# Interleaving the mask and score matmuls of two 64-column halves in a chunked attention kernel

## The chip, the cores and the metric

The kernel runs on one core of a Trainium2 chip. The metric is the device time of one execution in microseconds.

## The reference

Two layers, on x and ctx of shape 32 x 128 x 1024 (batch, channels, places). The first is attention within chunks of 64 places, 8 heads of 16 channels, then a projection, a residual and a normalisation over the places. The second finds for each place its 30 nearest places by the first channels of ctx, makes weights from their relative positions with a small network whose batch norms span everything, and adds the weighted neighbours' rows. Cut to what the change touches:

```python
qh, kh, vh = proj(q, Wq, bq), proj(k, Wk, bk), proj(v, Wv, bv)        # N, nc, 64, H, Dh
scores = jnp.einsum('bnqhd,bnkhd->bnhqk', qh, kh) * scale
km = masks[:, 0, :].reshape(N, nc, CHUNK)
scores = scores + jnp.where(km[:, :, None, None, :] > 0, 0.0, NEG)
attn = jax.nn.softmax(scores, axis=-1)
out = jnp.einsum('bnhqk,bnkhd->bnqhd', attn, vh)
...
pd = 2.0 * jnp.einsum('bdn,bdm->bnm', p, p) - xx[:, :, None] - xx[:, None, :]
idx = jax.lax.top_k(pd, k)[1]
```

## The kernel before

Three stages follow one another. Stage a (to about 4030 us of the span) loops over the 32 batches, and in a batch over 8 tiles t of 128 places (two chunks of 64 each). It computes the attention and the neighbour search together, by orders written out by hand for each engine, with semaphores between them. Stages b and e, the network and the weighted sum, do not touch the code of the change.

In stage a, VectorE (DVE) searches. For a pair of tiles it takes four rounds of 8 maxima over 1024 distances (MAX8 L866, FIND_INDEX8 L871, MATCH_REPLACE8 L873). In between it does, for the attention, the negated maximum of the scores (`largest`, L896), the reciprocal of the softmax sums (`inverse`, L900), and once in a half batch the digits of the indices (`digits`, L827 to L835). The distances stand in `pd_sb`, a ring of four tiles, which ScalarE (ACT) fills from PSUM in two halves a tile (L588).

TensorE (PE) walks per tile t through: the distances of tile t + 2, first half; second half; `scores` of tile t + 1; the transpose of tile t - 1's probabilities (L453); its values (L463); and on some tiles the output rows (L568), the value projection (L425), the query and key projection (L416) and the squares. Between these stand units of a neighbour gather for the batch before (L482, L503). So the distances of tile 7 come behind the scores of tile 5, those of tile 5 behind the scores of tile 3, and those of tile 3 behind the scores of tile 1. ACT walks through the same order, with the exponents (L754) between the two halves of the distances.

`scores(b, par, t)` waits for `exp_ready` (ACT has read the scores of the tile before, since `s_ps` is one bank) and for `kz_ready` (GpSimd, POOL, has spread the keys over the heads, L1115). It then makes four matmuls into `s_ps`, two for each half e of its 128 output partitions: a mask matmul of 32 rows x 64 columns in bf16 (L440), which starts the sum, and a score matmul of 128 rows x 64 columns in fp32 (L444), which adds to it. The last one raises `s_ready`, for which DVE's `largest` and POOL's key spreading two tiles on wait. The two halves use the same 32 or 128 rows, and different columns, of the array. An fp32 matmul stands in the trace as two records.

POOL spreads the keys of tile t + 1, multiplies the probabilities of tile t - 1 by the reciprocals (L1091), and does its share of the gather (L958 to L965) and of the spherical coordinates. At t = 3, from the third batch on, come 16 steps `sph_signs` (L987 to L1003) ahead of the spreading for tile 5.

Of the kernel before, what the change touches and what calls it, by code (L numbers as in the profile page):

```python
# [25 lines left out]
HEADS, CHUNK = 8, 64  # L26
# [7 lines left out]
QT = TILES // QUADS  # L34
# [111 lines left out]
def stage_a(nc, x, ctx, mask, w_in, b_in, w_out, b_out, consts, y_dram, cst, con, planes, idx_all, stats_all):  # L146
    OHR = 3
    XR = 97
    with ExitStack() as st:
        def sb(name, shape, dt=F32):  # L150
            return st.enter_context(nc.sbuf_tensor(name, shape, dt))
# [40 lines left out]
        qs = sb("qs", [P, HALF])  # L192
        kt = sb("kt", [P, HALF])
        kz = sb("kz", [P, 2, 2, HEADS, CHUNK])
# [11 lines left out]
        s_ps = st.enter_context(nc.psum_tensor("s_ps", [P, HEADS, CHUNK], F32))  # L206
# [154 lines left out]
        def _(pe):  # L361
            pe.wait_ge(w_in_landed, 96)
            for g in range(4):
                m = nc.tensor.transpose(mi_ps[0][:, g * C:(g + 1) * C], wnat[:, g, :], con["ident"])
# [64 lines left out]
            def scores(b, par, t):  # L429

                s = b * TILES + t

                if not (isinstance(s, int) and s == 0):
                    pe.wait_ge(exp_ready, s)
                pe.wait_ge(kz_ready, s + 1)
                if t == 0:
                    pe.wait_ge(minv_ready, b + 1)
                for e in range(2):
                    keys = minv[:, par, (2 * t + e) * CHUNK:(2 * t + e + 1) * CHUNK]
                    nc.tensor.matmul(s_ps[64 * e:64 * e + 64], negs[MASKS],  # L440
                                     keys.rearrange("p (o k) -> p o k", o=1).to_broadcast([32, HEADS, CHUNK]),
                                     start=True, stop=False)
                for e in range(2):
                    m = nc.tensor.matmul(s_ps[64 * e:64 * e + 64], qs[:, bass.ts(2 * (t % QT) + e, CHUNK)], kz[:, t % 2, e],  # L444
                                         start=False, stop=True)
                m.then_inc(s_ready, 1)

# [60 lines left out]
            def emit(b, j, par, first, last):  # L508
                misc = Misc(misc_base(b), first_bank(b, par))
                turned = None  # L510
                for t in range(TILES):
# [28 lines left out]
                    if quarter < QT - 1:  # L540
                        scores(b, par, t + 1)
                    elif ongoing:
                        scores(nb, npar, (t + 1) % TILES)
# [29 lines left out]
            for t in range(2):  # L573
                for h in range(2):
                    distances(0, 0, t, h)
            queries_keys(misc0, 0, 0)
            scores(0, 0, 0)
            batches(pe, emit)
            tail = Misc(TAIL, TAIL % 2)
# [1439 lines left out]
```

## Time and profile before

| what | value |
|---|---|
| median of 3 runs | 5792.33 us (5790.41 to 5798.28) |
| the profiled execution | 5790.41 us, span 5788.3 us |
| mean granted TensorE clock | 0.882 |
| busy share of the span | DVE 89%, PE 77%, ACT 70%, POOL 53%, PE weight loads 46% |

A PE at 77% is not 77% of its peak, since matmul ends are modelled and matmuls overlap. Busy shares are means over all three stages; what an edit costs is read from the waits in its own stage. L12 is line 12 of the kernel; PEld is TensorE's weight load.

### The profile page before, as it was taken

To read this page: it belongs to the slowest core of one execution; us is meant where nothing else is said; L and a number is where in the kernel's file an instruction comes from. 1 tells how busy PE (TensorE), PEld (TensorE's weight loads), DVE (VectorE), ACT (ScalarE), POOL (GpSimd) and SP (SyncE) were. 2 spreads that over 40 slices of the span, in tenths; PEclk is the share of its full clock that TensorE was granted. 3 is DMA by queue.
4 is the path that set the end of the run, shared out by engine and by line. 5 is a ranking of instruction groups with operands and counts; after the bars stand their busy time and mean duration, and the time that the engine had idled before them with its cause. 6 is when DMAs were issued, how large, how long until landed. Compare 5 with 4: busy or idle time off the path is not lost. (4 is left out here: it accounts for less than half of the span.)

```text
span 5788.3 us, 168890 instructions
## 1 busy us (share of the span) xinstructions
PE 4441.9 (77%) x62610; PEld 2689.3 (46%) x63182; DVE 5158.6 (89%) x7549; ACT 4026.4 (70%) x9505; POOL 3040.9 (53%) x3780
## 2 busy tenths in 40 slices
PE   6777777777777777777777777776395889899989
PEld 2444444444444444444444444443242666666666
DVE  7999999999989999998999998997398988888887
ACT  3777777777777777777777777776533766676666
POOL 3577777777777777777777777776400000000000
PEclk7988889888888898888888888897697999999999
DMA  0010000010000001000001000000000000000000
GB/s 29 16 31 16 16 17 17 17 31 16 17 16 17 17 17 31 16 17 16 17 17 31 17 16 17 16 16 12 1 0 8 25 30 27 30 26 30 27 30 26
DMA packets 135798, 114.60 MB, mean 20 GB/s; under 512 B 105344, under 2 KB 106112, under 8 KB 134784
## 3 DMA queue, kind: packets, MB, share of 16 engines
q1 hardware_dynamic: 134912, 102.73, 6.1%
q8 instruction: 563, 9.22, 0.7%
q14 instruction: 323, 2.65, 0.2%
HBM read 69.16 MB, written 33.55 MB: 18 GB/s over the span
## 5 line engine op out<-in xcount | busy, mean ns | idle before, releaser
L866 DVE MAX8 vals<-pd_sb 128x8 f32<-128x1024 f32 x1024 | 1199.8, 1210 | 270.2 <-ACT pd_sb L588 253.9
L588 ACT ACTIVATE ohT<-oh_ps 128x512 bf16<-128x512 f32 x1920 | 1152.2, 615 | 371.2 <-remote 209.7
L871 DVE FIND_INDEX8 idx<-vals,pd_sb 128x8 uint16<-128x1024 f32 x1024 | 1243.4, 1217 | 0.0
L503 PEld LDWEIGHTS g_ps<-tparts,ohT 128*128 128x128 bf16 x23040 | 871.6, 99 | 381.9 <-issue 152.4
L503 PE MATMUL g_ps<-tparts,ohT 128*128 128x24 bf16 x23040 | 883.4, 175 | 86.1 <-issue 46.9
L873 DVE MATCH_REPLACE8 pd_sb<-vals,pd_sb 128x1024 f32<-128x1024 f32 x768 | 927.4, 1207 | 0.0
L1955 PEld LDWEIGHTS e_a_ps<-planes,e_oh 120*128 120x128 bf16 x24576 | 687.2, 98 | 300.7 <-issue 219.8
L482 PE MATMUL oh_ps<-bitsT,code 128*128 128x512 bf16 x1348 | 584.2, 438 | 294.2 <-ACT bitsT L772 154.8
L1725 ACT COPY e_at<-e_a_ps 128x512 f32<-128x512 f32 x512 | 542.9, 1060 | 358.1 <-PE e_a_ps L1955 352.3
L1955 PE MATMUL e_a_ps<-planes,e_oh 120*128 120x32 bf16 x24576 | 702.4, 178 | 85.2 <-DVE e_oh L1883 46.9
L407 PE MATMUL pd_ps<-ctx_s 128*128 128x512 f32 x1024 | 656.1, 727 | 76.7 <-ACT pd_sb L588 74.8
L754 ACT ACTIVATE sS<-s_ps,mx 128x64 f32<-128x64 f32 x2048 | 609.0, 327 | 142.4 <-DVE mx L896 141.6
L1883 DVE TENSOR_TENSOR e_oh<-e_pairs,e_iotan 120x2048 bf16<-120x2048 bf16 x512 | 623.7, 1219 | 3.0 <-PE e_a_ps L1955 1.4
L482 PEld LDWEIGHTS oh_ps<-bitsT,code 128*128 128x128 bf16 x1920 | 193.7, 104 | 872.4 <-issue 396.9
L961 POOL TENSOR_TENSOR gsb<-gsb 128x240 f32<-128x240 f32 (+2 forms) x1152 | 543.4, 472 | 90.3
L1115 POOL TENSOR_TENSOR kz<-kt,cst 128x1024 f32<-128x1024 f32 x256 | 486.6, 1901 | 157.9 <-ACT kt L588 102.9
L1969 PE MATMUL e_o_ps<-e_at,e_xT 128*128 128x512 f32 x1024 | 568.3, 650 | 0.2 <-ACT e_at L1725 0.2
L1091 POOL TENSOR_TENSOR sS<-sS,rs 128x512 f32<-128x512 f32 x256 | 277.7, 1085 | 446.8 <-DVE rs L900 446.7
L440 PE MATMUL s_ps<-xp,negs 32*64 32x512 bf16 x512 | 115.1, 443 | 512.8 <-ACT sS L754 259.0
L588 ACT ACTIVATE pd_sb<-pd_ps,nxx 128x512 f32<-128x512 f32 x512 | 365.2, 713 | 198.5 <-PE pd_ps L409 198.3
L754 ACT ACTIVATION_READ_ACCUMULATOR sS<-s_ps,mx 128x1 f32 x2048 | 451.6, 221 | 0.0
L958 POOL TENSOR_TENSOR gsb<-gsb,hi1h 128x480 f32<-128x480 f32 x384 | 438.6, 1142 | 23.1 <-DVE hi1h L835 19.2
(241 smaller groups left out, 7381.1 us busy)
## 6 DMA issues: line engine op xcount, KB each, us to landing
ctx_s<-in_ctx SPq DMA_DIRECT2D x32, 512.0 KB, 4.3
maskb<-in_mask_Bx1x_ff SPq DMA_DIRECT2D x32, 512.0 KB, 6.4
x_s<-in_x SPq DMA_DIRECT2D x32, 512.0 KB, 5.7
y_spill<-y_s SPq DMA_DIRECT2D x32, 512.0 KB, 3.0
e_y<-y_spill SPq DMA_DIRECT2D x32, 512.0 KB, 4.1
out<-e_o SPq DMA_DIRECT2D x64, 256.0 KB, 2.2
table<-in_ctx SPq DMA_DIRECT2D x96, 4.0 KB, 5.8
pd_sb<-in_shape_constants SPq DMA_DIRECT2D x1, 1180.0 KB, 5.3
```

What stands on the lines that cost most here:

```text
L407: nc.tensor.matmul(pd_ps[:], ctx_s[:, par, bass.ts(t, P)], ctx_s[:, par, bass.ts(h, HALF)], start=True, stop=False)
L482: nc.tensor.matmul(oh_ps[k % 2][:], code[:, k % KT, :], bitsT[:, k // KT, :], start=True, stop=True).then_inc(oh_ready, 1)
L503: m = nc.tensor.matmul(found_ps[gi % 2][:, k % GK, t, :], ohT[:, k % OHR, bass.ts(t, P)], tparts[:, par, part, :], start=(part == 0), stop ...
L588: return nc.scalar.activation(dst, src, func, scale=scale, bias=bias)
L754: m = nc.scalar.activation(sS[:, t % 2, hd, :], s_ps[:, hd, :], ACT.Exp, bias=mx[:, t % 2, hd:hd + 1], accum_out=rs[:, t % 2, hd:hd + 1])
L866: nc.vector.max(vals[:, i, :], pd_sb[:, (t + i) % RING, :]).then_inc(topk_step, 1)
L871: found = nc.vector.max_index(idx16[:, par, t + i, 8 * r:8 * r + 8], vals[:, i, :], work)
L873: nc.vector.match_replace(work, vals[:, i, :], work, REMOVED).then_inc(topk_step, 1)
L961: steps(nc.gpsimd.tensor_tensor(sums[:, :, 0:width], sums[:, :, 0:width], sums[:, :, width:2 * width], ALU.add))
L1883: v.tensor_tensor(oh[pp, g % RING], low.to_broadcast([QCOLS, NB // 2, LO, 2]), row.to_broadcast([QCOLS, NB // 2, LO, 2]), ALU.is_equal).th ...
L1955: m = nc.tensor.matmul(a_ps[g % 2][:, i].rearrange("p t e -> p (t e)"), oh[pp, g % RING, i // 2, :, i % 2], spr[q][pp, part, :, (g * NB + ...
L1969: m = nc.tensor.matmul(o_ps[q][:], xT[:, par, e, :], at[:, q, e].rearrange("p t n -> p (t n)"), start=(e == 0), stop=(e == HI - 1))
```

## The change

Within `scores`, the four matmuls are issued in another order. Before: mask of half 0, mask of half 1, scores of half 0, scores of half 1. After: mask of half 0, scores of half 0, mask of half 1, scores of half 1. The operands, the waits and the semaphore on the last matmul stay.

```diff
                 for e in range(2):
+                    ch = 2 * (t % QT) + e
                     keys = minv[:, par, (2 * t + e) * CHUNK:(2 * t + e + 1) * CHUNK]
                     nc.tensor.matmul(s_ps[64 * e:64 * e + 64], negs[MASKS],
                                      keys.rearrange("p (o k) -> p o k", o=1).to_broadcast([32, HEADS, CHUNK]),
                                      start=True, stop=False)
-                for e in range(2):
-                    m = nc.tensor.matmul(s_ps[64 * e:64 * e + 64], qs[:, bass.ts(2 * (t % QT) + e, CHUNK)], kz[:, t % 2, e],
+                    m = nc.tensor.matmul(s_ps[64 * e:64 * e + 64], qs[:, bass.ts(ch, CHUNK)], kz[:, t % 2, e],
                                          start=False, stop=True)
                 m.then_inc(s_ready, 1)
```

## Rows read from the trace of the kernel before

**Rows 1.** The page: busy share of DVE in tenths, 40 slices of the span.
```profile
DVE  7999999999989999998999998997398988888887
```

**Rows 2.** Waits of DVE, 340 to 4030 us: total, times, longest.
```profile
DVE vals L866 <- ACT pd_sb L588: 226.6, 30, 8.4
```

**Rows 3.** Waits of PE in the same stretch, the two ahead of scores.
```profile
PE s_ps L440 <- POOL kz L1115: 248.1, 87, 5.4
PE s_ps L440 <- ACT sS L754: 217.7, 146, 3.6
```

**Rows 4.** Timeline of one call of scores (start, length): PE and PEld, 2000.3 to 2002.2.
```profile
2000.48 0.40 PE L440 MATMUL s_ps<-xp,negs 32*64 32x512 bf16 x2 [1.58 <-POOL kz L1115]
2000.81 0.20 PEld L444 LDWEIGHTS s_ps<-kz,qs 128*64 128x64 f32 x4 [0.23 <-issue]
2000.81 1.08 PE L444 MATMUL s_ps<-kz,qs 128*64 128x512 f32 x4
2001.82 0.10 PEld L482 LDWEIGHTS oh_ps<-bitsT,code 128*128 128x128 bf16 x1 [0.81 <-issue]
```

**Rows 5.** Timeline of one fp32 matmul of 128 x 128 x 512, PE.
```profile
2007.63 1.10 PE L407 MATMUL pd_ps<-ctx_s 128*128 128x512 f32 x2
```

**Rows 6.** Timeline, PE and PEld, elsewhere: shape kept, then shape changed.
```profile
2002.35 0.63 PE L453 MATMUL mi_ps<-cst,sS 128*128 128x128 f32 x4
2002.71 0.10 PEld L482 LDWEIGHTS oh_ps<-bitsT,code 128*128 128x128 bf16 x1
2002.82 0.38 PE L482 MATMUL oh_ps<-bitsT,code 128*128 128x512 bf16 x1
...
1973.74 1.35 PEld L425 LDWEIGHTS mi_ps<-wT,ctx_s 128*64 128x64 f32 x24 [0.76 <-issue]
```

**Rows 7.** Timeline of another call of scores (tile 6), PE and PEld.
```profile
1987.21 0.64 PE L440 MATMUL s_ps<-xp,negs 32*64 32x512 bf16 x2 [4.63 <-POOL kz L1115]
1989.68 0.10 PEld L482 LDWEIGHTS oh_ps<-bitsT,code 128*128 128x128 bf16 x1 [1.61 <-issue]
```

**Rows 8.** Timeline from the keys of tile 5 to DVE's wait, all engines.
```profile
1965.33 1.90 POOL L1115 TENSOR_TENSOR kz<-kt,cst 128x1024 f32<-128x1024 f32 x1 [0.25 <-POOL turn L1003]
1967.38 0.40 PE L440 MATMUL s_ps<-xp,negs 32*64 32x512 bf16 x2 [2.60 <-POOL kz L1115]
1969.58 0.60 ACT L588 ACTIVATE ohT<-oh_ps 128x512 bf16<-128x512 f32 x1 [2.79 <-remote]
1973.93 0.69 ACT L588 ACTIVATE y_s<-mi_ps,bias 128x512 f32<-128x512 f32 x1 [0.81 <-PE mi_ps L568]
1984.79 0.74 ACT L588 ACTIVATE pd_sb<-pd_ps,nxx 128x512 f32<-128x512 f32 x1
1985.67 1.23 DVE L866 MAX8 vals<-pd_sb 128x8 f32<-128x1024 f32 x1 [7.05 <-ACT pd_sb L588]
```

**Rows 9.** Stretch: busy PE, PEld, DVE, ACT, POOL, clock, DMA share, GB/s.
```profile
1968.80:1971.90 3.10, 2.77 (x47) 2.31 (x46) 3.10 (x5) 1.67 (x4) 2.68 (x6) 0.51 0.00 0
```

**Rows 10.** Timeline of the keys of tile 4, POOL.
```profile
1939.00 1.90 POOL L1115 TENSOR_TENSOR kz<-kt,cst 128x1024 f32<-128x1024 f32 x1 [2.47 <-ACT kt L588]
1942.31 1.04 POOL L1091 TENSOR_TENSOR sS<-sS,rs 128x512 f32<-128x512 f32 x1 [1.40 <-DVE rs L900]
1944.16 1.36 POOL L1125 CAST bitsb<-bits 128x896 bf16<-128x896 uint16 x1 [0.82 <-DVE bits L827]
```

**Rows 11.** Timeline: scores of tile 1, distances of tile 3, DVE's use of them.
```profile
1904.13 1.98 PE L444 MATMUL s_ps<-kz,qs 128*64 128x512 f32 x4
...
1918.56 0.74 ACT L588 ACTIVATE pd_sb<-pd_ps,nxx 128x512 f32<-128x512 f32 x1
...
1921.42 1.21 DVE L866 MAX8 vals<-pd_sb 128x8 f32<-128x1024 f32 x1
```

**Rows 12.** Timeline: DVE's maxima over the scores of tile 6.
```profile
1991.69 0.64 DVE L896 TENSOR_REDUCE mx<-s_ps 128x8 f32<-128x512 f32 x1
```

## The prediction

> **What bounds the kernel now.** I read the page first. Its slices of DVE [rows 1] show nine tenths or more in nearly every slice of stage a, so stage a is as long as DVE's work plus DVE's waits, and the change lies in stage a alone. The second view is the waits of DVE in stage a's steady part [rows 2]: one wait is left that matters, before the first maximum over a tile's distances, 226.6 us in 30 times, so 7.55 us each. Nothing on DVE waits for the scores themselves in this stretch. The third view, the timeline, says where in a batch the wait falls and what leads to it [rows 8]: it is the first use of tile 7's distances, and these come behind tile 5's scores on PE. The chain is: POOL ends its spherical steps, spreads the keys of tile 5 (start 1965.33, 1.90 us), PE starts the scores at 1967.38, ACT's next one-hot waits 2.79 us for PE, later its output rows wait 0.81 us for PE, and behind the value copies, one table load and eight exponents ACT ends the distances at 1985.53 (1984.79 + 0.74); DVE starts 0.14 us later. Each link waits for the one before, so a call of scores that takes longer here makes this wait longer by the same. It occurs once a batch, for the 30 batches in which POOL has the spherical steps (batches 2 to 31).
>
> The fourth view, the waits of PE [rows 3], says the opposite of the other calls. In 240 calls of this stretch PE stood waiting before the scores, 248.1 us for keys (87 times) and 217.7 us for ACT's exponents (146 times), both of which hang on DVE or POOL. There a longer call eats the slack of the next call's wait.
>
> **The change, part by part.** Nothing is added: four matmuls and the same weight loads stand in another order. What it can remove is overlap. Today's call [rows 4]: the two masks start together (one row, x2, 0.40 us long), the four score records begin 0.33 us later and are through 1.08 us after that, and the load that follows starts at 2001.82. So the call costs 2001.82 - 2000.48 = 1.34 us. The four score records are two fp32 matmuls of 64 columns; one of 128 columns takes 1.10 us alone [rows 5]. So the two halves run beside each other and one half alone would take as long as both.
>
> Do they still meet in the new order? Between the two score matmuls there now stands a mask matmul of another shape (32 rows, not 128). What the trace shows of a change of shape: where the shape stays, the next weights are loaded during the matmuls before (L482's load at 2002.71, while L453 runs, its own matmul at 2002.82, [rows 6]). Where it changes, they are not: L444's load starts 0.33 us after the masks' start and with its own matmul, after PEld had stood idle 0.23 us; L482's after the scores with 0.81 us idle [rows 4]; L425's (64 columns, after 128) with 0.76 us idle [rows 6]. All are put down to "issue", that is, to nothing that a semaphore shows. I read this as PE emptying itself before it changes shape. In the new order the shape changes after every matmul, so nothing overlaps: mask 0.33, scores 1.01, mask 0.33, scores 1.01, together 2.68 us. The cost of a call is +1.34 us at the full clock (2.4 GHz). The same call at the half clock (1.2 GHz) takes 1989.68 - 1987.21 = 2.47 us [rows 7], so there it costs up to +2.47 us.
>
> The Trainium skill says the same in "TensorEngine Tiling (Array Packing)", Key Properties: changing the tiling mode, not just the tile, drains TensorE. By that rule the halves cannot meet and each call costs its own length again. The trace agrees, by the idle weight loads above.
>
> *On the path.* The 30 calls for tile 5: 30 x 1.34 = 40.2 us, if PE is at the full clock; 30 x 2.47 = 74.1 us at the half clock. In the batch shown the clock was 0.51 from 1968.8 to 1971.9 [rows 9], just behind the call. I take 40.2: if the slow stretch lies where it lay, the added work fills a part of it and pushes the same amount of other PE work to where the clock is full, so the end of the chain moves by the full-clock price.
>
> *Two places with little slack.* (1) Tile 3's distances were in place at 1919.30 and first read at 1921.42 [rows 11]; less the 0.14 us of the handover that leaves 1.98 us. They come behind tile 1's scores, which here ran at the half clock (L444 1.98 us long, against 1.08 at the full clock). At the full clock the +1.34 fits, at the half clock 0.49 us is lost. (2) The keys of tile 4 wait for kt, which comes behind tile 3's scores; behind them POOL has 1.40 + 0.82 = 2.22 us of waits for DVE before its gather and the spherical steps [rows 10]. +1.34 fits; +2.47 pushes 0.25 us on into the chain of tile 5. Both in every batch would be 30 x 0.74 = 22 us. I take 10, since calls run at either clock.
>
> *Hidden.* The other calls. Tile 6's scores start when POOL's keys are there, 4.63 us after PE had run dry [rows 7], and are through by the next load at 1989.68; DVE reads them at 1991.69 [rows 12], 2.0 us later, and DVE itself comes later by tile 5's price (at least 1.34), so even +2.47 is covered. If that cover were gone, it would cost the difference once a batch. Tiles 0, 2, 4 and 7 have PE's own waits of rows 3, on average 465.8 / 233 = 2.0 us each, behind them.
>
> Sum, against the profiled execution's 5790.4 us: + 40.2 + 10 = 5840.6. That execution lies 1.9 us under the median of the three, so I predict 5842 us.
>
> **The rivals.**
> 1. *The halves still overlap (not slower).* The column halves are different parts of the array, and if each has its own queue, the new order gives half 0 (mask, scores) beside half 1 (mask, scores), again 1.34 us. For it: the first passes of both halves start together although the second pass of half 0 was issued before half 1 [rows 4], so matmuls of different halves are not bound to the order of issue. Against it: the idle weight loads at every change of shape. It decides if a 32-row and a 128-row matmul may be in the array together. Time 5792 us. In between, the second mask runs beside the first scores and only its 0.33 us is added: 30 x 0.33 = 10 us, 5802.
> 2. *The half clock spreads.* Every call on the path costs 2.47 us and both thin places give way: 74.1 + 22 = 96 us, 5888. For it: the clock fell to about a half around two of the calls shown [rows 7, 9]. Against it: fuller PE stretches give the clock fewer idle stretches to fall after.
> 3. *The clock gains.* PE idles less before the call of tile 5, since tile 4's price fills part of its wait (2.60 us before the call, [rows 8]), so calls that ran at 2.47 now take 2.68 in two parts at the full clock, +0.21 only. If half of the 30 do so: 15 x 0.21 + 15 x 1.34 = 23 us, 5815.
>
> **How the numbers follow.** Serialising in any form has 0.86: as forecast 0.69, rival 3 0.10, rival 2 and beyond 0.07. Rival 1 has 0.14, 0.04 of it in its halfway form. The range goes from 5812, under rival 3, to 5880, where most but not all calls are at the half clock; it leaves out rival 1 and the end of rival 2. A measurement of this kernel tells 0.2% (11.6 us) from no change. Slower by over 0.2%: 0.84, the 0.86 less 0.02 for a serialising whose price nearly vanishes in the clock; faster: 0.03, out of rival 1, for a clock that rises with nothing serialised; within: 0.13, the rest of rival 1 and those 0.02.
>
> **What would show it.** Right: a call of scores shows six matmul records in four steps, 2.68 us from first mask to next load at the full clock, its busy sum in the group of L444 about doubled; DVE's wait for pd_sb 30 times with about 9 us each instead of 7.55; PE's waits before L440 shorter. The step on thin slack is right if a few new DVE waits of under 1 us stand at tile 3. Wrong: masks and scores of the halves in pairs (rival 1); DVE waiting for `s_ps` before L896, which would mean that I misjudged tile 6; or a stage b and e of other length, where nothing is changed.

## The result and the profile after

| | before | after |
|---|---|---|
| median of 5 runs | 5795.02 us | 5822.19 us (5817.2 to 5827.9) |
| profiled execution, span | 5788.3 us | 5829.4 us |
| mean granted clock | 0.882 | 0.908 |

The ratio is 1.0052, 95% interval 1.0040 to 1.0064: slower by 0.5%, some 30 us. The forecast was 5842 us (5812 to 5880). The direction and the doubling of the call came out as predicted; the sum was 20 us too high, since its largest term was more than twice too large. The profiled execution of before lies 5 us under the median of its runs and that of after 9 us above, so the terms below sum to 41 us and not to 27.

Of each view only the rows that matter are shown, word for word. First the call of scores in the timeline, PE and PEld, at the full clock (start, length, idle before; the loads of L444 are left out). It answers to [rows 4]:

```profile
1985.72 0.37 PE L441 MATMUL s_ps<-xp,negs 32*64 32x512 bf16 x1 [2.42 <-POOL kz L1115]
1986.03 1.07 PE L444 MATMUL s_ps<-kz,qs 128*64 128x512 f32 x2
1987.03 0.10 PEld L441 LDWEIGHTS s_ps<-xp,negs 32*64 32x64 bf16 x1 [0.81 <-issue]
1987.03 0.40 PE L441 MATMUL s_ps<-xp,negs 32*64 32x512 bf16 x1
1987.36 1.07 PE L444 MATMUL s_ps<-kz,qs 128*64 128x512 f32 x2
1988.36 0.10 PEld L482 LDWEIGHTS oh_ps<-bitsT,code 128*128 128x128 bf16 x1 [0.81 <-issue]
```

Four steps stand where there were two: mask, scores, mask, scores. The second mask's weights are loaded when the first scores are through, after 0.81 us of idle put down to "issue". From the first load, at 1985.69 in the same view, to the next of another line at 1988.36 it is 2.67 us, against 1.34 before.

The waits of DVE (total, times, longest), from 340 us on, answer to [rows 2]; then the same view from 30 to 340 us:

```profile
DVE vals L866 <- ACT pd_sb L588: 262.6, 40, 10.0
DVE vals L866 <- issue: 17.0, 12, 1.9
...
DVE vals L866 <- ACT pd_sb L588: 30.7, 5, 21.7
DVE mx L896 <- PE s_ps L444: 3.6, 1, 3.6
```

Before, these were 226.6 us in 30 times, and 27.3 us in 3 times with 0.8 us for the scores. Going through the 40 waits one by one in the timeline, 30 are those for tile 7's distances, 244.3 us together, 8.14 us each against 7.55. The other ten are new: 18.3 us for tile 3's distances, the longest 4.7 us. So the rise of 36.0 us is 17.7 at tile 7 and 18.3 at tile 3. The first two batches add 6.2 us.

The waits of PE before the scores, same stretch, answer to [rows 3]:

```profile
PE s_ps L441 <- ACT sS L754: 129.2, 172, 2.1
PE s_ps L441 <- POOL kz L1115: 118.1, 55, 4.3
```

247 us of waiting where there were 466: 219 of the 329 us that the 240 calls take more (by the table below) came out of PE's own waits. PE's idle time shrinks and the clock rises. The view by stretch, of stage a's steady part, before and after (busy PE, PEld, DVE, ACT, POOL, then the granted clock):

```profile
333.00:4018.00 3685.00, 2746.85 (x32947) 1566.07 (x33476) 3436.02 (x4994) 2731.60 (x7755) 2786.85 (x3466) 0.87 0.07 18
```

```profile
333.00:4058.00 3725.00, 3069.48 (x33543) 1573.44 (x33541) 3438.51 (x5007) 2740.93 (x7773) 2800.23 (x3475) 0.91 0.07 18
```

PE works 323 us more and the clock goes from 0.87 to 0.91. From the starts of the 30 calls for each tile to the next load of another line, the mean lengths of a call are (us):

| tile | 0 | 1 | 2 | 3 | 4 | 5 | 6 | 7 |
|---|---|---|---|---|---|---|---|---|
| before | 1.34 | 1.61 | 1.40 | 1.78 | 1.37 | 2.05 | 2.29 | 1.51 |
| after | 2.66 | 2.69 | 2.66 | 2.70 | 3.61 | 2.83 | 4.33 | 2.84 |

Tile 5's call, the one on the path, became 0.78 us longer, not 1.34 or 2.47. It used to run partly at the half clock (1.2 GHz): the mean granted clock over the call was 0.67, and 14 of the 30 calls took over 2.4 us. Now 27 of 30 take 2.63 to 2.66 us, at a mean clock of 0.96.

The call is only one part of the path from POOL's keys to ACT's last copy of tile 7's distances. Worked out from the timelines of the same 30 batches, means in us:

| | keys ready to start of the call | the call | end of the call to distances in place |
|---|---|---|---|
| before | 0.14 | 2.05 | 16.64 |
| after | 0.65 | 2.83 | 15.94 |

The call starts 0.51 us later, since in 12 of the 30 batches PE, held up by the longer calls before it, comes after the keys (in experiment 3, where those are short, it never does); it is 0.78 us longer; and what follows it is 0.70 us shorter. That is the 0.59 us a batch by which the wait grew.

The new waits at tile 3, in the batch where the longest stands. Timeline of PE, ACT and DVE:

```profile
2042.92 1.03 PE L474 MATMUL mi_ps<-identb,bitsb 128*128 128x128 bf16 x8 [3.57 <-issue]
2047.30 2.05 PE L407 MATMUL pd_ps<-ctx_s 128*128 128x512 f32 x2
2052.93 0.40 PE L441 MATMUL s_ps<-xp,negs 32*64 32x512 bf16 x1 [0.52 <-ACT sS L754]
2062.66 1.10 PE L407 MATMUL pd_ps<-ctx_s 128*128 128x512 f32 x2
2067.40 0.75 ACT L588 ACTIVATE pd_sb<-pd_ps,nxx 128x512 f32<-128x512 f32 x1
2068.28 1.23 DVE L866 MAX8 vals<-pd_sb 128x8 f32<-128x1024 f32 x1 [4.69 <-ACT pd_sb L588]
```

The batch begins with PE idle for 3.57 us with nothing to wait for, ahead of L474. This stands at the head of the hand-written loop over pairs of batches, at each of its 12 returns to the head, and in before as well (42.6 us in 12 times against 43.7). Behind it PE ran at the half clock (the first L407 took 2.05 us) and came to the calls for tiles 1 and 2 with only the handover of 0.5 us to spare. Before, PE still waited 1.62 us on average ahead of tile 1's call, and now 0.43, so I read it that the same delay was taken up by those waits and is no longer. Nine of the ten waits at tile 3 stand in a batch that opens this loop. In experiments 4, 8 and 12 too, twelve waits stand in the twelve batches that open it. That the delay at the loop's head makes them is argued from these places; no run took it away.

### The profile page after: what moved, and what is told of

The parts are those of the page before. It is cut to its first block and busy times, and to the rows that moved or that the text cites. A ratio compares the mean times of both kernels' runs of the same rounds, so it can differ in the third digit from the quotient of the medians.

```text
span 5829.4 us, 169462 instructions
## 1 busy us (share of the span) xinstructions
PE 4784.7 (82%) x63182; PEld 2694.6 (46%) x63182; DVE 5153.9 (88%) x7549; ACT 4027.0 (69%) x9505; POOL 3047.6 (52%) x3780
## 5 line engine op out<-in xcount | busy, mean ns | idle before, releaser
L866 DVE MAX8 vals<-pd_sb 128x8 f32<-128x1024 f32 x1024 | 1201.0, 1210 | 310.8 <-ACT pd_sb L588 293.4
L503 PEld LDWEIGHTS g_ps<-tparts,ohT 128*128 128x128 bf16 x23040 | 851.5, 97 | 347.5 <-issue 103.1
L482 PE MATMUL oh_ps<-bitsT,code 128*128 128x512 bf16 x1920 | 777.8, 411 | 284.9 <-ACT bitsT L772 154.0
L503 PE MATMUL g_ps<-tparts,ohT 128*128 128x24 bf16 x23040 | 869.3, 174 | 3.3
L407 PE MATMUL pd_ps<-ctx_s 128*128 128x512 f32 x1024 | 661.7, 732 | 75.4 <-ACT pd_sb L588 73.6
L444 PE MATMUL s_ps<-kz,qs 128*64 128x512 f32 x1024 | 639.5, 710 | 0.0
L441 PE MATMUL s_ps<-xp,negs 32*64 32x512 bf16 x512 | 221.0, 432 | 278.0 <-ACT sS L754 157.1
```

Of the source, the lines that this page charges most:

```text
L407: nc.tensor.matmul(pd_ps[:], ctx_s[:, par, bass.ts(t, P)], ctx_s[:, par, bass.ts(h, HALF)], start=True, stop=False)
L482: nc.tensor.matmul(oh_ps[k % 2][:], code[:, k % KT, :], bitsT[:, k // KT, :], start=True, stop=True).then_inc(oh_ready, 1)
L503: m = nc.tensor.matmul(found_ps[gi % 2][:, k % GK, t, :], ohT[:, k % OHR, bass.ts(t, P)], tparts[:, par, part, :], start=(part == 0), stop ...
L866: nc.vector.max(vals[:, i, :], pd_sb[:, (t + i) % RING, :]).then_inc(topk_step, 1)
```

## The experiments

Each was timed against the kernel before on its own chip, so experiments are compared by their ratios. All numbers of tiles are worked out over the same 30 batches as above.

**1. One shape, in the new order.** The mask matmul takes all 128 rows, with weights that are zero outside its three.

```diff
-                    keys = minv[:, par, (2 * t + e) * CHUNK:(2 * t + e + 1) * CHUNK]
-                    nc.tensor.matmul(s_ps[64 * e:64 * e + 64], negs[MASKS],
-                                     keys.rearrange("p (o k) -> p o k", o=1).to_broadcast([32, HEADS, CHUNK]),
+                    keys = xp[:, par, (2 * t + e) * CHUNK:(2 * t + e + 1) * CHUNK]
+                    nc.tensor.matmul(s_ps[64 * e:64 * e + 64], negs[:],
+                                     keys.rearrange("p (o k) -> p o k", o=1).to_broadcast([P, HEADS, CHUNK]),
```

> The new order, but the mask matmul takes all 128 rows (weights are zero outside its three rows, so the sums are the same), so that mask and score matmuls have one shape, 128 x 64. Theory (a change of shape empties PE): the halves meet again, a call costs 1.34 us or less, DVE's wait before tile 7's distances is back near 7.5 us x 30, no new waits at tile 3; time within 6 us of before. Rival (the order of issue alone serialises, whatever the shape): a call stays at 2.66 us at the full clock and the time near that of the changed kernel, +27 us. Halfway (the second mask waits for the first scores' second part to start): a call near 2.1 us, +10 us.

Measured: 5787.66 us, ratio 0.9998 (0.9989 to 1.0007). Its timeline of a call, PE:

```profile
2010.90 0.41 PE L441 MATMUL s_ps<-xp,negs 128*64 128x512 bf16 x2 [0.51 <-ACT sS L754]
2011.14 1.03 PE L444 MATMUL s_ps<-kz,qs 128*64 128x512 f32 x4
2012.11 0.39 PE L482 MATMUL oh_ps<-bitsT,code 128*128 128x512 bf16 x1
```

The order of issue is that of the slower kernel, and yet the two masks start together (x2) and the four score records run in pairs: 2012.11 - 2010.90 = 1.21 us for the call. DVE's waits are back at 218.8 us in 30 times, 7.8 less than before; DVE's digits, to which experiment 3 comes, take 5.7 us more. So neither the order nor the accumulation serialises the halves. The change of shape does. The scores now start 0.24 us after the masks, not 0.33. This settles rival 1 of the prediction: the halves can go on beside each other out of the order of issue, but only as long as the shape stays.

**2. One shape, in the order of before.** The same edit in the kernel before.

> The order of before with 128-row masks. Theory (a change of shape empties PE): the step from masks to scores falls from 0.33 us to about 0.23 us, a call from 1.34 to about 1.23 us; time as before, 0 to -5 us. Rival (the 0.33 us is needed by the accumulation into the same place): the call stays at 1.34 us, time as before.

Measured: 5786.15 us, ratio 0.9995 (0.9986 to 1.0004). At the full clock tile 5's call takes 1.19 us. A change of shape between masks and scores therefore cost 0.10 to 0.15 us a call even where it was grouped. Of the kernel's time this is less than can be measured: the wait at tile 7 fell by 6.1 us (220.5 against 226.6), and DVE's digits took 11.2 us more (198.1 against 186.9).

**3 and 4. Which call pays.** The new order for tile 5 alone, and for all tiles but 5, by a condition on t in `scores`. There mask(e) and score(e) make the two matmuls of a half as before, which puts DVE's and ACT's lines 11 further down (L877 is L866). The edit, without these two definitions:

```diff
+                if t == 5:          # experiment 3; t != 5 in experiment 4
+                    for e in range(2):
+                        mask(e)
+                        m = score(e)
+                else:
+                    for e in range(2):
+                        mask(e)
+                    for e in range(2):
+                        m = score(e)
```

> The new order for tile 5's call alone. Theory (the other calls' longer PE work keeps the clock up, which paid back part of tile 5's price): without them the call of tile 5 often runs at the half clock, mean 3.4 to 4.1 us instead of 2.83, the wait before tile 7's distances grows by 1.3 to 2.05 us a batch, +40 to +60 us in all, more than the whole change costs. Rival (the price of tile 5's call is 0.6 us on the path for another reason, such as slack in the chain): +18 us, and no waits at tile 3.

> The new order for all tiles but 5. Theory (the others give the clock back and cost at tile 3): tile 5's call falls from a mean of 2.05 to about 1.45 us, the wait before tile 7's distances shrinks by 0.6 us a batch, -18 us, against +18 us of waits at tile 3 and +7 us in the first two batches: +7 us in all. Rival (tile 5's call alone is the price, the others are hidden and change no clock): 0 us at tile 7, +25 us from tile 3 and the first two batches.

Measured, tile 5 alone: 5804.32 us, ratio 1.0025 (1.0016 to 1.0034), about +14 us. All but tile 5: 5803.33 us, ratio 1.0025 (1.0014 to 1.0037). Waits of DVE from 340 us on, in the first and in the second:

```profile
DVE vals L877 <- ACT pd_sb L599: 273.3, 30, 10.2
```

```profile
DVE vals L877 <- ACT pd_sb L599: 262.8, 51, 9.3
DVE vals L877 <- issue: 11.4, 9, 1.5
DVE mx L907 <- PE s_ps L445: 8.5, 21, 0.7
```

The part about the clock came out as the theory had it, in direction. With the other calls short, tile 5's call took 4.16 us on average, +2.11, and the wait at tile 7 grew by 46.7 us, which is 1.56 a batch. With the other calls long and tile 5's short, that call took 1.34 us every time, 0.71 less than in before, and the wait at tile 7 fell to 212.6 us, 14 less. So the long calls elsewhere do pay back part of tile 5's price. The time before and behind the call shows the same parts as above: with the other calls long it starts 0.75 us after the keys and 16.28 us follow it; with them short, 0.15 and 16.19. At tile 3 the long calls cost 46.5 us in 18 waits here, 12 of them in the batches that open the loop.

The time did not come out for tile 5 alone: +14 us, with 47 us more waiting at tile 7. DVE's busy time in stage a must have fallen, and the view of instructions by line shows where. Groups of DVE instructions (busy, mean ns), first before, then tile 5 alone:

```profile
L827 DVE TENSOR_TENSOR bits<-idx,bitval 128x896 uint16<-128x896 uint16 x64 | 83.5, 1305 | 16.2 <-POOL planes L965 16.2
L835 DVE TENSOR_TENSOR hi1h<-hi,hival 128x960 bf16<-128x960 uint16 x64 | 60.3, 942 | 2.2
L831 DVE TENSOR_SCALAR hi<-idx 128x120 uint16<-128x120 uint16 x64 | 43.1, 674 | 0.0
```

```profile
L838 DVE TENSOR_TENSOR bits<-idx,bitval 128x896 uint16<-128x896 uint16 x64 | 76.1, 1190 | 16.9 <-POOL planes L976 16.9
L846 DVE TENSOR_TENSOR hi1h<-hi,hival 128x960 bf16<-128x960 uint16 x64 | 48.2, 754 | 2.2
L842 DVE TENSOR_SCALAR hi<-idx 128x120 uint16<-128x120 uint16 x64 | 26.1, 408 | 0.0
```

The same three digit instructions, of the same shapes, take 186.9 us in one and 150.4 us in the other: 36.5 us come back there. With all calls but tile 5's long they take 151.1 us, 35.8 less than before, and without that its profiled execution would, by estimate, be 47 us longer than before's, not 12. In the changed kernel they take 179.5 us, 7.4 less than before.

**5. Where the waits at tile 3 come from.** The condition is `t > 1`, so that tiles 0 and 1 keep the order of before.

> The new order for all tiles but 0 and 1 (measured at the changed kernel: +0.52%, +30 us). Theory (the new waits at tile 3 and the loss in the first two batches come of PE lagging behind tiles 0 and 1): no waits at tile 3 (18 us there before in 10 batches), the first two batches within 3 us of before's, tile 7's waits as in the changed kernel (244 us); +8 to +15 us on the kernel before. Rival (the waits at tile 3 come of the calls of the batch's end before it, whose price runs on): still 10 or more waits at tile 3, +25 us or more.

Measured: 5804.19 us, ratio 1.0023 (1.0011 to 1.0034), about +13 us. One wait of 2.1 us is left at tile 3, tile 7's are 243.0 us. The waits at tile 3 come of the calls for tiles 0 and 1, as the theory had it.

**6 and 7. The keys of tile 5 earlier.** POOL spreads them ahead of the spherical steps, in the kernel before and in the changed one.

```diff
-                    if t % QT != QT - 1:
+                    if t % QT != QT - 1 and t != QT:
                         spread_keys(b, t + 1)
...
                     if t == 3:
+                        spread_keys(b, QT + 1)
                         if there(b - 3):
                             sph_turn(b - 3)
```

> The kernel before, with POOL spreading tile 5's keys ahead of the 16 spherical steps instead of behind them. Theory (the wait at tile 7 is the end of the chain keys of tile 5, scores of tile 5, distances of tile 7): tile 5's scores start about 2.2 us earlier, when ACT's exponents are done, and tile 7's wait falls from 7.5 to about 5.5 us a batch, less what new waits for the scores of tile 6 take back: -30 to -60 us. Rival (the wait hangs on POOL or ACT work behind the scores): the wait stays within 0.5 us of 7.5, time the same.

> The changed kernel with the same early keys. Theory (there PE itself comes late: only 1.00 us of wait is left before tile 5's scores, against 3.13 in the kernel before): the gain is 0.5 to 0.8 us a batch, -15 to -25 us on the changed kernel, so about +5 to +15 us on the kernel before, and DVE waits for the scores of tile 6. Rival (the price is independent of where the keys come): it gains as much as the kernel before does, so it stays 30 us behind that one, at -30 to 0 us on the kernel before.

Measured: 5781.93 us, ratio 0.9980 (0.9971 to 0.9989), and 5814.57 us, ratio 1.0036 (1.0022 to 1.0049). In the kernel before the call for tile 5 did start as soon as ACT let it (0.31 us of idle on average, against 3.13), and ran at the full clock each time. But the wait at tile 7 did not shrink; it grew, to 247.3 us. My expectation was wrong, and the waits of PE in that kernel say why:

```profile
PE mi_ps L453 <- POOL sS L1092: 48.3, 30, 3.9
PE mi_ps L568 <- ACT oT L588: 45.3, 59, 1.7
```

PE now waits 30 times behind the scores for POOL's multiplication of the probabilities (0.5 us in one time before), and after it for ACT's values (6.8 us in 37 times before). It stands in POOL's queue behind the same spherical steps and the same spreading, so only the order of two waits for POOL was turned round. The head of the chain in [rows 8] is POOL's work of that stretch as a whole, not the keys. The gain of 0.2% is that of the digits, 153.6 us against 186.9, less the 21 us that the wait grew. In the changed kernel the early keys gave 0.16% less time than the change alone, which is less than the theory's 15 to 25 us, and with the two intervals overlapping it may be nothing. Its wait at tile 7 did fall as the theory had it, by 16.2 us (228.1 against 244.3), and DVE now waits for scores, nearly all of them tile 6's (5.7 us in 15 times). Counted from DVE's first use of tile 4's distances, tile 5's call starts 1.0 us sooner there, and what follows it takes 0.6 us more.

**8 and 9. The digits.** DVE's digits of tiles 0 to 3 moved, in the kernel before, ahead of the reciprocal and the maxima (8), and between them, with the maxima first (9). The edit of 9; that of 8 puts `digits` alone ahead of both:

```diff
-                        if r % 2 == 0:
+                        if t == 6 and r == 2:
+                            largest(s + 1, t + 1)
+                            digits(b, par, 0)
+                            inverse(s, t)
+                        elif r % 2 == 0:
                             if r > 0 or t > 0 or not first:
...
                         if t == 6 and r == 2:
-                            digits(b, par, 0)
                             row_stats(b, 0)
```

> The kernel before, with DVE's digits of the first half taken ahead of the reciprocal and the maxima of scores (at tiles 6 and 7's third round) instead of behind. Theory (the three digit instructions run long when a POOL tensor-tensor runs beside them, 1.66, 1.14 and 1.23 us against 0.62, 0.29 and 0.66; the reciprocal starts POOL's multiplication just then): the three fall from 3.77 us to 2.2 to 2.8 us, -30 to -45 us in all. Rival (their length is their own, and the shorter ones in other kernels are chance of alignment elsewhere): 3.77 us stays, time the same; or the later reciprocal delays POOL and PE and the gain is taken back by waits.

> The kernel before, with DVE's digits of the first half between the maxima of scores (first) and the reciprocal (last) at the place where digits_first had them ahead of both. Theory (POOL's multiplication, started by the reciprocal, is what lengthens the digits; and the new waits at tile 3 in digits_first, 18.6 us, came of the late maxima): the digits take 2.4 to 2.9 us as there, the waits at tile 3 go away, -35 to -45 us on the kernel before. Rival (the waits at tile 3 come of the late reciprocal, since PE's transpose waits for POOL behind it): the waits stay, -20 us as digits_first.

Measured: 5773.13 us, ratio 0.9964 (0.9952 to 0.9976), and 5747.65 us, ratio 0.9918 (0.9904 to 0.9931). The timeline shows the cause. In the kernel before, DVE and POOL:

```profile
2008.47 1.76 DVE L827 TENSOR_TENSOR bits<-idx,bitval 128x896 uint16<-128x896 uint16 x1
2010.16 1.14 DVE L831 TENSOR_SCALAR hi<-idx 128x120 uint16<-128x120 uint16 x1
2011.33 1.26 DVE L835 TENSOR_TENSOR hi1h<-hi,hival 128x960 bf16<-128x960 uint16 x1
...
2007.86 1.90 POOL L1115 TENSOR_TENSOR kz<-kt,cst 128x1024 f32<-128x1024 f32 x1
2009.72 1.42 POOL L1091 TENSOR_TENSOR sS<-sS,rs 128x512 f32<-128x512 f32 x1
2011.08 1.00 POOL L1125 CAST bitsb<-bits 128x896 bf16<-128x896 uint16 x1
```

In kernel 9:

```profile
1992.89 1.45 DVE L827 TENSOR_TENSOR bits<-idx,bitval 128x896 uint16<-128x896 uint16 x1
1994.27 0.29 DVE L831 TENSOR_SCALAR hi<-idx 128x120 uint16<-128x120 uint16 x1
1994.59 0.66 DVE L835 TENSOR_TENSOR hi1h<-hi,hival 128x960 bf16<-128x960 uint16 x1
...
1991.96 1.90 POOL L1118 TENSOR_TENSOR kz<-kt,cst 128x1024 f32<-128x1024 f32 x1 [0.68 <-ACT kt L588]
1995.44 1.04 POOL L1094 TENSOR_TENSOR sS<-sS,rs 128x512 f32<-128x512 f32 x1 [1.57 <-DVE rs L903]
```

Where POOL stands idle, L831 takes 0.29 us and L835 0.66; beside POOL's multiplication and cast they take 1.14 and 1.26, and POOL's multiplication itself 1.42 instead of 1.04. The reciprocal is what starts that multiplication. Over the 32 uses the three together fall from 3.77 to 2.42 us, 43 us in all, and the time fell by 47. The Trainium skill states a rule for this ("SBUF — State Buffer", the section on its two separate sides): DVE and GpSimd share a pair of ports as an exclusive lock, which a DVE instruction in a two-port mode, or one with two SBUF inputs against a GpSimd instruction that reads SBUF, holds or waits for as a whole. The lengths above agree with blocking, on both engines; whether all of each longer length is the lock, no run here shows.

In kernel 8, 13 waits of 18.7 us together appeared at tile 3, 12 of them in the batches that open the loop; in kernel 9 none. The theory had this too: in 8 the maxima, and with them the exponents and PE's calls, came late.

**10. Kernel 9 with one shape.**

> digits_between with 128-row masks in the grouped order (a call of scores 1.19 us instead of 1.34 at the full clock). Theory (the call's length counts at tile 5, and at tile 3 where slack is thin): 0.15 us a batch at tile 5 and up to that at tile 3, -5 to -10 us on digits_between, that is -25 to -55 us on the kernel before. Rival (the clock takes it back): as digits_between within 3 us.

Measured: 5751.05 us, ratio 0.9924 (0.9910 to 0.9937), not to be told from kernel 9. The wait at tile 7 is 10.8 us shorter (221.1 against 231.9), and DVE is 8.5 us busier, mostly in L835 (0.99 us on average in place of 0.66). What the shorter call gave, the timing of the digits took, as in experiment 2.

**11 and 12. The new order on top of kernel 9.** Tile 5 alone (11), all tiles (12).

> only5 and digits_between together. In only5 DVE's waits grew by 50 us and the time by 16 us only; the digit instructions were 36 us shorter there. Theory (that was a payback by chance of timing: DVE's digits fell beside less POOL work; with the digits moved there is little left to pay back): this kernel is 35 to 50 us slower than digits_between, so at 0 to -12 us on the kernel before. Rival (the payback lies elsewhere): 16 us slower than digits_between, -30 us on the kernel before.

> The change and digits_between together. The change cost +30 us on the kernel before, with about 8 us paid back by shorter digits. Theory: +35 to +45 us on digits_between here, so -2 to -12 us on the kernel before, with tile 3's waits in 10 batches or more since digits_between leaves 4.3 us instead of 5.8 us of slack for tile 1's distances. Rival (the costs of the order of calls do not add up with the place of the digits): +30 us or less on digits_between, -17 us or less on the kernel before.

Measured: 5787.09 us, ratio 0.9990 (0.9981 to 0.9999), and 5813.93 us, ratio 1.0036 (1.0022 to 1.0050). Against kernel 9 (0.9918) tile 5's call now costs 0.0072, that is 42 us, where it cost 14 us in experiment 3. The profiled executions are 35 us apart. This goes with a smaller payback, but it was not gone as my theory had it. The digits of the kernels 9 and 11:

```profile
L827 DVE TENSOR_TENSOR bits<-idx,bitval 128x896 uint16<-128x896 uint16 x64 | 83.3, 1302 | 16.4 <-POOL planes L968 16.4
L835 DVE TENSOR_TENSOR hi1h<-hi,hival 128x960 bf16<-128x960 uint16 x64 | 42.1, 658 | 2.2
L831 DVE TENSOR_SCALAR hi<-idx 128x120 uint16<-128x120 uint16 x64 | 18.5, 290 | 0.0
```

```profile
L838 DVE TENSOR_TENSOR bits<-idx,bitval 128x896 uint16<-128x896 uint16 x64 | 63.6, 993 | 16.2 <-POOL planes L979 16.2
L846 DVE TENSOR_TENSOR hi1h<-hi,hival 128x960 bf16<-128x960 uint16 x64 | 42.1, 658 | 2.2
L842 DVE TENSOR_SCALAR hi<-idx 128x120 uint16<-128x120 uint16 x64 | 18.7, 292 | 0.0
```

They still give back 19.5 us (143.9 against 124.4), nearly all of it in L827, where experiment 3 gave back 36.5. The waits at tile 7 grow by 47.9 us, much as there, and 3.6 us are new at tile 3.

The whole change on top of kernel 9 costs 0.0118, 68 us, more than either theory said; the profiled executions are 62 us apart, with the digits 11.0 us shorter. The waits of DVE for distances are 237.1 us at tile 7, and 53.3 us in 13 waits at tile 3, twelve of them of 3.9 to 4.9 us, in the twelve batches that open the loop. The timelines show that kernel 9 was closer to this edge. In before, tile 3's distances were in place 2.0 to 2.1 us ahead of their first use in each of the 30 batches; in kernel 9, only 0.7 to 1.8 us in the twelve that open the loop. So the costs of the order of calls and of the place of the digits do not add up.

## Why the prediction was right, and where its sum was off

**A call doubles.** Right in mechanism and size: 2.68 us predicted, 2.66 measured at the full clock; experiment 1 shows that the change of shape is the cause. Rival 1 is out.

**30 x 1.34 us at tile 5.** The step that was mis-sized. It measured 0.59 us a batch, 17.7 us. I argued that the price on the path is that of the full clock since the slow stretch would keep its place. It did not stay: PE's idle time before the call fell from 3.13 to 1.00 us, and the mean clock over it rose from 0.67 to 0.96. I had this as rival 3, with 0.10, priced at 0.21 us for half of the calls; experiments 3 and 4 show it (4.16 and 1.34 us for the call with the others short and long). Two parts I had nowhere: the call starts 0.51 us later, and what follows it is 0.70 us shorter. On this term the truth lay with rival 3 (23 us) and even below it, not with the forecast. The total lay between the two, 5822 us against 5815 and 5842, since the thin places and the first two batches cost more than I had put. That the total fell into the range is in part luck: 22.5 us too much on the largest term, 14.5 us too little on those two.

**Thin slack.** The two places were put at 10 us; the waits at tile 3 were 18.3 us in 10 batches. The place was right, and so was that tile 1's call leads there; experiment 5 shows the calls for tiles 0 and 1 as the cause. The size was not: I expected waits of under 1 us from tile 1's call at the half clock, and it ran at the full one; the waits were 1.8 us on average and up to 4.7. Where they stand points at the 3.6 us of idle at the loop's head, which is in PE's waits of before and which I passed over. The keys of tile 4 cost nothing that can be made out: those of tile 5, behind them on POOL, come at the same time after DVE's first use of tile 4's distances (16.84 and 16.87 us).

**Hidden calls.** Right for tiles 6 and 7: DVE waited 0.2 us in all for the scores of tile 6. The first two batches, which the sum left out, cost 6.2 us.

**Not in the sum at all:** that DVE's own instructions change length when its work shifts against POOL's. It gave back 7 us in the changed kernel and 36 us in each of experiments 3 and 4.

The rows of the profiled execution give 17.7 + 18.3 + 6.2 - 7.4 = 34.8 us, and 3 us more in the loop's issue waits and behind stage a, of the 41.1 us between the spans. DVE's other instructions of stage a are some 2 us longer in sum, which leaves 1 us. Whether early keys help the changed kernel at all stays open.

One reading of the rows was not as sure as I wrote it: the 2.79 us of wait ahead of ACT's one-hot in [rows 8] stand there as "remote", and that it waits for PE is my inference from what it reads.

## What to carry to other kernels

Group matmuls on TensorE by their shape: here those on different columns ran beside each other in either order of issue while the shape stayed, and not at all across a change of it. Before pricing a longer instruction on an engine with idle gaps, ask what the gaps do to its clock: here more work elsewhere made the one call on the path, and the work behind it, cheaper. And where a change shifts two engines against each other, compare busy times too, not waits alone; the best kernel here (0.8% faster than before) came from moving three DVE instructions out of the way of one on POOL.

## What the runs showed of the hardware that I had not expected

- Matmuls of the two column halves are not held to the order of issue: with one shape, mask 1 starts with mask 0 though a two-part fp32 matmul was issued between them (experiment 1).
- A DVE instruction on 16-bit data can take four times its length beside POOL work: 0.29 us alone, 1.14 us beside a multiplication, which itself went from 1.04 to 1.42 us.
- At the head of a loop that is not unrolled, PE stood idle 3.3 to 3.9 us and DVE up to 1.9 us with nothing to wait for, at each of the 12 returns to the head of a loop of 13 rounds. What fills this time no run shows.
